# Attention weights split in pieces with semaphores of their own, and the first blocks of two feed-forward phases in another order

## The reference, cut to what matters

```python
x = x + 0.5 * ffn(layernorm(x))
x = x + attn(layernorm(x))
x = x + 0.5 * ffn(layernorm(x))

def ffn(x):                                  # 8 experts, top 2
    logits = x @ router_w + router_b
    vals, idx = top_k(logits, 2)
    full_w = sum(one_hot(idx, 8) * softmax(vals)[..., None], axis=-2)
    h = silu(einsum('td,edf->etf', x, expert_w) + expert_b[:, None])
    combined = einsum('etf,te->tf', h, full_w)
    y = x + combined @ proj_w + proj_b
    return norm_w * y / sqrt(mean(y * y) + 1e-6)

def attn(x):                                 # 16 heads, 4 key/value heads of 128
    q, k, v = x @ wq.T, x @ wk.T, x @ wv.T   # split in heads, rope on q and k
    p = softmax(causal(q @ (k * key_weights).T / sqrt(128)))
    return (p @ v) @ wo.T
```

## Time and profile before

| | |
|---|---|
| median of three runs | 867.75 us (866.32 to 869.53) |
| the profiled execution, in all | 870.1 us |
| its span, first to last instruction | 867.2 us |
| PE busy | 803.8 us (93%) |
| DVE busy | 679.8 us (78%) |
| ACT busy | 503.6 us (58%) |
| POOL busy | 484.8 us (56%) |
| phase 1, attention, phase 2 start at | 0, 169, 734 us |

### The profile page before, as it was taken

One profiled execution on the slowest core, in us unless ns is written; L12 is line 12 of the kernel. 1 busy time (PEld: TensorE's weight loads), 2 busy tenths in 40 slices (PEclk: granted clock), 3 DMA queues, 4 the chain that ended last, 5 costly groups with the idle time before them and its releaser, 6 DMA issues. The chain is left out here.

```text
span 867.2 us, 16033 instructions
## 1 busy us (share of the span) xinstructions
PE 803.8 (93%) x4712; PEld 703.5 (81%) x4712; DVE 679.8 (78%) x1948; ACT 503.6 (58%) x1241; POOL 484.8 (56%) x382
## 2 busy tenths in 40 slices
PE   7897897867899999999999999999999998799995
PEld 4676676655799999999998998999999997688884
DVE  6887898599966877868768768768778797888874
ACT  3434544445665766767758558657667674445442
POOL 4312331268577787777877877877877751212211
PEclk9998998979999999999999999999999999899997
DMA  9040451410112312312212212132121100000001
GB/s 306 3 173 16 176 183 48 115 44 13 37 30 69 97 24 48 83 38 73 73 36 58 75 36 73 24 97 49 56 65 30 40 17 1 1 1 25 25 1 49
DMA packets 25238, 52.18 MB, mean 60 GB/s; under 512 B 3442, under 2 KB 9202, under 8 KB 23922
## 3 DMA queue, kind: packets, MB, share of 16 engines
q1 hardware_dynamic: 25204, 51.77, 20.9%
HBM read 19.77 MB, written 11.01 MB: 35 GB/s over the span
## 5 line engine op out<-in xcount | busy, mean ns | idle before, releaser
L1147 DVE TENSOR_TENSOR at_ptl<-at_pt,at_pth 128x512 fp32r<-128x512 f32 (+1 forms) x192 | 108.8, 593 | 45.0 <-ACT at_pth L1293 44.9
L1293 ACT ACTIVATE at_pth<-at_pt 128x512 fp32r<-128x512 f32 (+1 forms) x192 | 94.2, 525 | 85.6 <-PE at_pt L1451 85.6
L1287 ACT ACTIVATE at_pr<-at_pr,at_low 128x512 f32<-128x512 f32 (+3 forms) x256 | 140.5, 557 | 2.3 <-DVE at_low L1133 2.2
L1035 POOL TENSOR_TENSOR at_ql<-at_rot,at_qh 128x512 fp32r<-128x512 f32 x62 | 79.7, 1285 | 98.1 <-ACT at_qh L1272 98.1
L602 ACT ACTIVATE f_ex<-f_ex 128x512 f32<-128x512 f32 x128 | 74.1, 583 | 86.4 <-PE f_ex L766 86.2
L445 DVE SCALAR_TENSOR_TENSOR f_acc<-f_ex,f_full,f_acc 128x256 f32<-128x256 f32 x224 | 95.9, 476 | 33.4 <-ACT f_ex L602 32.7
L1142 DVE TENSOR_SCALAR at_pr<-at_pr,at_inv 128x128 f32<-128x128 f32 (+3 forms) x256 | 110.5, 492 | 2.3
L1050 POOL TENSOR_TENSOR at_rot<-at_rot,gc 128x512 f32<-128x512 f32 x78 | 101.4, 1300 | 8.1 <-POOLq L1067 2.1
L1044 POOL TENSOR_TENSOR at_rot<-ga,cos 128x512 f32<-128x512 f32 x78 | 101.9, 1307 | 4.1 <-POOL at_ql L1035 2.4
L1451 PE MATMUL at_pt<-ident,at_pr 128*128 128x128 f32 x640 | 94.1, 278 | 9.5 <-DVE at_pr L1142 8.6
L1046 POOL TENSOR_TENSOR gc<-gc,sin 128x512 f32<-128x512 f32 x78 | 102.3, 1312 | 0.0
(11 more groups left out here) (212 smaller groups left out, 2130.8 us busy)
## 6 DMA issues: line engine op xcount, KB each, us to landing
gc<-ga SPq DMA_DIRECT2D x160, 128.0 KB, 2.3
ga<-in_attn_w SPq DMA_DIRECT2D x4, 1280.0 KB, 7.1
at_wo<-attn_split SPq DMA_DIRECT2D x8, 512.0 KB, 4.1
attn_split<-gb SPq DMA_DIRECT2D x3, 1280.0 KB, 9.8
attn_split<-gc SPq DMA_DIRECT2D x3, 1280.0 KB, 12.4
gb<-attn_split SPq DMA_DIRECT2D x6, 512.0 KB, 4.2
x<-in_x SPq DMA_DIRECT2D x4, 512.0 KB, 9.3
e_raw<-in_expert_w SPq DMA_DIRECT2D x8, 256.0 KB, 6.0
```

The costliest lines, as they stand in the source:

```text
L1147: dve.tensor_tensor(ptl[h % 2][:, cols], pt[(NF * h + k) % 2][:, 0:FLEN[k]], pth[h % 2][:, cols].bitcast(F32), ALU.subtract).then_inc(lo_d ...
L1287: act.activation(pr[h % 2][:, cols], pr[h % 2][:, cols], ACT.Exp, bias=low[h % 2][:, i:i + 1], scale=-1.0, accum_out=tot[h % 2][:, i:i + 1 ...
L1293: act.activation(pth[h % 2][:, cols], pt[(NF * h + k) % 2][:, 0:FLEN[k]], ACT.Copy).then_inc(hi_done, 1)
```

## The change

It loads, splits and stores a group in four pieces, of 768, 768, 512 and 512 columns, with a semaphore for each piece's loads and stores; six slots move. On POOL the wait for the load is per piece. In phase 1 the first block is reordered on all four engines, and three small constants are computed on POOL instead of DVE. In phase 2 DVE does `pair_rest(2)` ahead of `weigh_chosen(0)` instead of in `body(0)`, and POOL's `residual(0)` waits for it.

```diff
+        ORDER = (1, 2, 3, 0)
+        EDGES = (0, QKV, C * QKV, C * QKV + G * D // 2, GW)
+        PIECES = len(EDGES) - 1
...
             ident_in, x_in, e_row_in = sem("ident_in"), [sem(f"x_in{n}") for n in range(BATCH)], sem("e_row_in")
-            a_in, a_scaled, a_hi_done, a_lo_done, a_out, wa_in = (sem(n) for n in ("a_in", "a_scaled", "a_hi_done", "a_lo_done", "a_out", "wa_in"))
+            a_in, a_out = ([sem(f"{n}{m}") for m in range(PIECES)] for n in ("a_in", "a_out"))
+            a_scaled, a_hi_done, a_lo_done, wo_out = (sem(n) for n in ("a_scaled", "a_hi_done", "a_lo_done", "wo_out"))
...
-        ORDER = (1, 2, 3, 0)
-        PIECES = 4
-        SLOTS = ((3, 4, 5, 6), (10, 11, 12, 13), (17, 18, 19, 20), (25, 26, 27, 28))
+        SLOTS = ((3, 4, 5, 6), (9, 10, 12, 13), (17, 18, 20, 21), (25, 26, 28, 29))
...
         def piece_at(i, g, p):
...
-        def group_piece(i, m):
...
-            if ORDER[i] > 0:
-                part = slice(m * GW // PIECES, (m + 1) * GW // PIECES)
+        def group_piece(k, m):
...
+            if ORDER[k] > 0:
+                part = slice(EDGES[m], EDGES[m + 1])
...
         def _(sp):
...
-            def load_group(i):
-                sp.dma_start(a_raw[:], d["attn_w"][ORDER[i]]).then_inc(a_in, 16)
...
-            def store_group(i):
-                sp.wait_ge(a_lo_done, PIECES * (i + 1))
-                load_group(i + 1)
-                sp.dma_start(split[ORDER[i], 0], a_hi[:].bitcast(F32)).then_inc(a_out, 16)
-                sp.dma_start(split[ORDER[i], 1], a_lo[:].bitcast(F32)).then_inc(a_out, 16)
+            def load_piece(k, m):
+                part = slice(EDGES[m], EDGES[m + 1])
+                sp.dma_start(a_raw[:, part], d["attn_w"][ORDER[k]][:, part]).then_inc(a_in[m], 16)
...
+            def store_piece(k, m):
+                part = slice(EDGES[m], EDGES[m + 1])
+                sp.wait_ge(a_lo_done, PIECES * k + m + 1)
+                sp.dma_start(split[ORDER[k], 0][:, part], a_hi[:, part].bitcast(F32)).then_inc(a_out[m], 16)
+                sp.dma_start(split[ORDER[k], 1][:, part], a_lo[:, part].bitcast(F32)).then_inc(a_out[m], 16)
...
             def load_block(b):
...
                 load_block(1)
-                load_group(0)
+                for m in range(PIECES):
+                    load_piece(0, m)
...
                 sp.dma_start(sinT[:], d["rope_sin"]).then_inc(tables_in, 16)
-                for i in range(KV - 1):
-                    store_group(i)
+                for k in range(KV - 1):
+                    for m in range(PIECES):
+                        store_piece(k, m)
+                        load_piece(k + 1, m)
...
                 for n in range(2):
-                    sp.dma_start(split[0, n, :, C * QKV:GW], a_lo[:, n * G * D:(n + 1) * G * D].bitcast(F32)).then_inc(a_out, 16)
-                sp.wait_ge(a_out, 32 * KV)
+                    sp.dma_start(split[0, n, :, C * QKV:GW], a_lo[:, n * G * D:(n + 1) * G * D].bitcast(F32)).then_inc(wo_out, 16)
+                for m in range(PIECES):
+                    sp.wait_ge(a_out[m], 32 * (KV - 1))
+                sp.wait_ge(wo_out, 32)
...
             def scale_queries(i):
...
                 k = ORDER[i]
-                pool.wait_ge(consts, 2)
-                pool.wait_ge(a_in, 16 * i + 16)
+                if i == 0:
+                    pool.wait_ge(consts, 2)
...
                     q = a_raw[:, c * QKV + HD:c * QKV + QKV - HD].rearrange("p (h d) -> p h d", h=G)
+                    pool.wait_ge(a_in[c], 16 * i + 16)
...
                 rstd(0)
+                pool.wait_ge(rows_in, 16)
+                pool.tensor_tensor(r_off[:], r_bias, r_first, ALU.subtract).then_inc(consts, 1)
+                pool.tensor_scalar(kw, kw, -float(HD) ** -0.5, None, ALU.mult).then_inc(consts, 1)
+                pool.tensor_scalar(n_w, n_w, 0.5, None, ALU.mult).then_inc(consts, 1)
...
                 shift_late(3)
-                pool.wait_ge(rows_in, 16)
+            else:
+                pool.wait_ge(e_lo_done, 3)
...
             def scale_rows(i, g):
                 dve.wait_ge(rr_done, 2 * i + g + 1)
+                if first and i == 0 and g == 0:
+                    dve.wait_ge(consts, 3)
...
                     norm_stats(1)
-                    if not first:
-                        pair_rest(2)
...
                 norm_stats(0)
+                norm_rows(0)
+                shift_pair(0)
...
                 dve.tensor_tensor(r_hl[:, :, E:2 * E], r_raw, r_hl[:, :, 0:E].bitcast(F32), ALU.subtract).then_inc(r_split, 1)
-                shift_pair(0)
-                norm_rows(0)
-                pair_rest(0)
...
                 z_rest(0)
+                pair_rest(0)
                 shift_pair(1)
-                dve.wait_ge(rows_in, 16)
-                dve.tensor_tensor(r_off[:], r_bias, r_first, ALU.subtract).then_inc(consts, 1)
-                dve.tensor_scalar(kw, kw, -float(HD) ** -0.5, None, ALU.mult).then_inc(consts, 1)
-                dve.tensor_scalar(n_w, n_w, 0.5, None, ALU.mult).then_inc(consts, 1)
-                dve.wait_ge(consts, 3)
+                dve.wait_ge(consts, 1)
...
             choose(0)
-            if first:
-                pair_rest(2)
+            pair_rest(2)
...
                     raw_part, hi, _ = group_piece(k, m)
-                    act.wait_ge(a_scaled, C * k + C)
-                    if k > 0 and (ORDER[k] > 0 or m > 0):
-                        act.wait_ge(a_out, 32 * k)
+                    if m < C:
+                        act.wait_ge(a_scaled, C * k + (m + 1 if ORDER[k] > 0 else C))
+                    elif ORDER[k] > 0:
+                        act.wait_ge(a_in[m], 16 * k + 16)
+                    elif m == PIECES - 1:
+                        act.wait_ge(a_in[2], 16 * KV)
+                        act.wait_ge(a_in[3], 16 * KV)
+                    if k > 0 and ORDER[k] > 0:
+                        act.wait_ge(a_out[m], 32 * k)
+                    elif ORDER[k] == 0 and m == 1:
+                        for other in range(3):
+                            act.wait_ge(a_out[other], 32 * k)
...
             def step_out(k):
...
             if first:
+                z_lead(0)
+                pair_lead(0)
                 row_out(2)
-                pair_lead(0)
-                row_out(3)
-                act.wait_ge(ident_in, 16)
-                z_lead(0)
...
             if first:
+                row_out(3)
...
                 pe.wait_ge(e_row_in, 16)
-                for p in range(PAIRS):
-                    row_of(p)
+                row_of(0)
+                row_of(1)
...
                 transpose_first_z()
+                row_of(2)
...
             router(0)
+            if first:
+                row_of(3)
```

## The result

The changed kernel takes 857.83 us (median of four runs, 856.77 to 858.36) beside 867.04 for the kernel before; the ratio is 0.989, 95% interval 0.9863 to 0.9916. The forecast was 857.3, worked out from the median of 867.75 that the kernel before had until then; a fourth run of it made that 867.04. The profiled execution has a span of 855.4 us.

What follows compares the result with a forecast made beforehand. It took PE and DVE, some 29 us of work each per block, plus waiting, chiefly ScalarE's for the gc store, as the bound. Terms +1.0 - 7.1 - 2.6 - 1.0 - 0.7 = -10.4 gave 857.3 us, range 851 to 863.

Steps and rivals of the forecast that it cites:

- The stalls: Blocks 1 and 2 of phase 1: pieces end both ScalarE waits for the gc store; block 1 -7.1 us.
- Block 2: Second block of phase 1: from 31.96 to 29.4 us, -2.6, with 1.0 us of DVE idle left.
- Slots of the last group: Block 3 of phase 1: z rows start earlier, behind a 512-wide piece; PE stops 3.6 instead of 4.60 us, -1.0.
- First block of phase 1: Start of phase 1: POOL holds pair_rest(1) and the gap subtraction; first weighted sum at 25.7 instead of 24.67, +1.0 us.
- The choice of the nearest row: First block of phase 1: gap subtraction assumed to wait for POOL, like the 8-column operation of 1.66 us.
- First block of phase 2: Start of phase 2: residual(0) meets weigh_chosen(0), yet PE goes on at 745.75 instead of 746.45, -0.7 us.
- The sum: Whole kernel: +1.0 - 7.1 - 2.6 - 1.0 - 0.7 = -10.4 us, giving 857.3 us.
- A: Rival, both first blocks and block 3: POOL collisions don't happen or the clock stays up; about 852 us, chance 0.22.
- B: Rival, blocks 1 and 2: freed time mostly lost to DVE, 31.5 us each; -7.0 in all, 860.8 us, chance 0.14.
- C: Rival, first blocks of both phases: slower, POOL holds DVE, first sum over 3 us later; 872.2 us, chance 0.04.
- D: Rival, piece waits: they still wait for whole-group stores, so no change; 867 us, chance 0.02.

Runs made afterwards that it cites:

- e1: Changed kernel with both first blocks back in their old order, so pieces, semaphores and moved slots alone; 857.31 us, 0.9872 of the kernel before.
- e2: Kernel before with only the new order of the two first blocks, groups whole and old slots; 868.49 us, 1.0009 of the kernel before.
- e4: Changed kernel, but ScalarE waits once, at a group's first piece, for the stores of the whole group before it; 857.45 us, 0.9876 of the kernel before.
- e3: Changed kernel with the old slots 25, 26, 27, 28 for the last group; 859.48 us, 0.9898 of the kernel before.
- e8: Changed kernel with slots 25, 26, 29, 30 for the last group, no piece before the z rows; 857.93 us, 0.9883 of the kernel before.
- e7: Changed kernel, but in phase 1 POOL's residual(0) waits until weigh_chosen(0) is done; 855.96 us, 0.9866 of the kernel before.
- e5: Changed kernel with phase 2 in its old order; 857.37 us, 0.9879 of the kernel before.
- e10: Changed kernel with POOL's residual(0) behind weigh_chosen(0) in both phases; 854.9 us, 0.9859 of the kernel before.
- e6: Changed kernel, but in phase 2 POOL's residual(0) waits until weigh_chosen(0) is done; 855.94 us, 0.986 of the kernel before.
- e12: e10 with slots 25, 26, 29, 30 for the last group; 854.15 us, 0.9836 of the kernel before.
- e9: Kernel before with only later slots for all groups but the first, groups still loaded and stored whole; 861.31 us, 0.9925 of the kernel before.

## Why the prediction was right

*The stalls.* Both ScalarE waits went, block 1 lost 7.0 us (forecast 7.1), with the clock at 1.00 throughout. e1 and e2 show that this and the slots are the whole gain. The working allowed sixteen microseconds for the landing of a piece; the last one of group 0 took 4.3 at most (e4).

*Block 2* lost 1.6 and not 2.6 us. The step that was mis-sized is DVE's idle outside the stall, taken as 1.0: DVE is busy 28.33 us of 30.34, so 2.0 are left, and in every version with pieces blocks 1 and 2 take 30.3. The 2.17 us of the 3.60 that were put down to the stall were PE's stop; DVE's own idle fell by 1.6 only. PE is busy for 29.05 and stops twice, 0.8 us for the last sums of a block and 0.4 for `z_rest`; no kernel here with pieces came down to 29.4. Block 1 came out right by two errors: DVE's idle was again 2.0 and not 1.0, but its busy time in the block fell from 29.18 to 28.31, 0.5 us of it in the four z rows (0.66 us each instead of 0.79), two of which took 2.25 us beside POOL's scaling before. That the two cancel is luck.

*Slots of the last group.* Forecast -1.0, measured -1.7 by e3. PE's stop was 3.48 us (forecast 3.6). The mechanism held, with the piece lengthened to 1.37 us by the row addition. The step that was off is the price of the clock, left in as before: PE works at the lower clock for 3.4 us instead of the 4.7 of e3, which is 0.6 of the missing 0.7. e8 shows that this addition is the next thing there.

*First block of phase 1.* First weighted sum at 25.89, forecast 25.7, and each link as worked out: `pair_rest(1)` held to 19.7 (forecast 19.1), the gap subtraction held by residual(0). The choice of the nearest row, the 8-column operation that waited, was right, and e7 shows it from the other side: without the residual the sum is at 24.52. This is the lock of the Trainium skill's "SBUF — State Buffer", section "Who interferes with whom"; the trace agrees, down to an operation on four columns that takes 1.50 us.

*First block of phase 2.* The collision came at the forecast place, though only one of the seven operations was held: 2.34 us in `weigh_chosen(0)`, the first sum 2.4 us later behind the router than before (9.75 against 7.39), and PE going on 1.0 us earlier (forecast 0.7). What that is worth was wrong: e5 shows 0, not -0.7, because the z rows behind DVE's sums and norm come 1.2 us later behind the router than in e5, PE stops for them again (0.54 us), and the first sum of the second half is 0.1 us later (24.21 against 24.09). The prediction had this in hand (the transposes "can start at" 750.9, with PE's units before them "as before") and counted the 0.7 all the same.

*The sum* came out by errors that cancel, which is luck: block 2 (1.0 too much) and phase 2 (0.7 too much) against the slots (0.7 too little) and block 0, whose 0.9 us were a term that the prediction didn't have. Those go with the pieces, not with the order: block 0 takes 29.74 us in e1 and 30.62 in e2 (of the other kernels with pieces it takes 29.7 in all but e4 and e10, 30.1 and 30.2 there). The traces name a wait. ScalarE's first piece now asks for the first of POOL's two scalings and not for both; the changed kernel, then e2:

```profile
36.76 0.85 ACT L642 ACTIVATE gb<-ga 128x768 fp32r<-128x768 f32 x1 [0.95 <-POOL ga L292]
```

```profile
37.84 0.74 ACT L623 ACTIVATE gb<-ga 128x640 fp32r<-128x640 f32 x1 [1.96 <-POOL ga L282]
```

From the first weighted sum that is 10.9 us, the same in e1, against 11.9. No run changes this wait alone, so it is read from the traces and not shown by experiment.

Of the rivals, A's price for phase 2 was reached in e6 (2.4 us) but not again in e10 and e12, and in the order of the changed kernel POOL does meet those operations; B, that DVE takes back the gain, holds for 1.0 us of it. C needed a first sum over 3 us later than before; it was 1.2 us later in phase 1 and 2.4 in phase 2. D is ruled out by the missing waits.

## What to carry to other kernels

When an engine that works in order waits for a store to land so that a buffer can be filled again, store each part as soon as it is done, so that only the last small one is still out; or move the turn of the buffer's next use behind the landing, one changed line, which gave up to 6.6 of 10.6 us here (e9, with the last group's turns moved too). A long GpSimd operation with its inputs in SBUF, released at the moment at which a chain of tiny VectorE operations begins, can cost that chain nearly its whole length (2.2 us by an operation of 2.36 us in phase 2, 1.3 in phase 1): release it behind the chain, beside work on PSUM. And a stop that is made shorter pays only if what follows it isn't late by as much; look at the next thing that both engines wait for.

## What the runs showed of the hardware that was not expected

The length of the lower clock behind the same stop of PE varies between executions (about 6 us and 3 us behind 4.29 us, above), so one profiled execution can hold 1.5 us that the next does not. Whether it falls behind a short stop varies as well: in phase 2 it fell behind 2.05 us in e10 and 2.07 in e12, and not behind 2.06 in e6. The start of attention is the other such place. PE stops and starts there for 50 us in all kernels, and attention as a whole took 564.7 to 566.6 us in twelve of the fourteen profiled executions of this study, but 562.55 in e2 and 561.89 in e10, with one and the same code. These two, and only they, had the lower clock already in the first 4 us. PE in two stretches of 2 us from the first matmul of attention, in e10, e2 and e12 (length, busy, granted clock):

```profile
157.77:159.77 2.00, 2.00 (x5) 0.54 0.49 120
159.77:161.77 2.00, 2.00 (x7) 0.61 1.01 382
```

```profile
171.23:173.23 2.00, 2.00 (x5) 0.54 0.56 125
173.23:175.23 2.00, 2.00 (x7) 0.61 1.01 401
```

```profile
157.16:159.16 2.00, 2.00 (x9) 1.00 0.38 101
159.16:161.16 2.00, 1.02 (x5) 1.00 1.05 399
```

So the two executions that began attention at the lower clock ended it some 3 us sooner. Why wasn't tried and stays open. For an effect of 2 us in this kernel two single profiles are not enough; e10's profiled run, 852.03 us, is the fastest of its five.
